# Next layer's weights in a six-layer stack: the cast to their high part moves from VectorE to ScalarE, and four groups of loads are issued one step later

## The reference, cut to what matters

```python
def attn_layer(x, Wqkv, qs, ksc, Wo):
    qkv = x @ Wqkv                      # 16 heads of 64
    q = l2norm(q) * qs
    k = l2norm(k) * ksc
    q = q * cos * scale + rotate_half(q) * sin * scale
    k = k * cos * inv + rotate_half(k) * sin * inv
    out = local_attention(q, k, v)      # windows of 32, each looks at 64 keys
    return out @ Wo
for i in range(DEPTH):                  # DEPTH = 6
    x = attn_layer(shift_tokens(x), Wqkv[i], q_scale[i], k_scale[i], Wo[i]) + x
    x = ffn_layer(shift_tokens(x), ln_g[i], ln_b[i], W1[i], b1[i], W2[i], b2[i]) + x
```

## Time and profile before

| what | us |
|---|---|
| median of three runs | 1199.79 (1198.54 to 1201.1) |
| the profiled execution, its own time | 1197.58 |
| its span, first to last instruction | 1195.8 |
| PE busy | 1116.0 (93%) |
| VectorE busy | 930.1 (78%) |
| ScalarE busy | 839.9 (70%) |
| GpSimd busy | 684.2 (57%) |
| mean granted TensorE clock | 0.983 of full speed |

### The profile page before, as it was taken

How to read it: one execution, slowest core, us unless ns; L and a number is a source line. 1 busy time by engine, 2 the same in 40 slices (tenths; PEclk the granted TensorE clock), 3 DMA queues, 4 the chain that set the end, 5 groups by cost and what they waited for, 6 DMA issues and landing times. The chain is left out here.

```text
span 1195.8 us, 26412 instructions
## 1 busy us (share of the span) xinstructions
PE 1116.0 (93%) x9694; PEld 711.2 (59%) x9694; DVE 930.1 (78%) x1367; ACT 839.9 (70%) x1340; POOL 684.2 (57%) x546
## 2 busy tenths in 40 slices
PE   9877889998868999999999999999999999999997
PEld 3222367785324776766666676666666676666662
DVE  3999868775538887888888787888888788888853
ACT  5655465664445787788877887788877887787853
POOL 2999655442526665755666565755656565755520
PEclk9989999999969999999999999999999999999999
DMA  5332162100303643535334443535344453544320
GB/s 168 107 96 96 36 194 74 39 14 1 106 0 88 156 115 82 130 96 150 95 102 120 124 121 82 129 99 154 87 104 119 122 126 79 127 103 110 92 69 18
DMA packets 81223, 117.48 MB, mean 98 GB/s; under 512 B 26003, under 2 KB 32594, under 8 KB 80714
## 3 DMA queue, kind: packets, MB, share of 16 engines
q1 hardware_dynamic: 80586, 115.03, 36.1%
q10 hardware_dynamic: 512, 0.80, 0.2%
HBM read 41.12 MB, written 0.72 MB: 35 GB/s over the span
## 5 line engine op out<-in xcount | busy, mean ns | idle before, releaser
L2061 POOL TENSOR_TENSOR st_sq_sum<-h 128x512 f32<-128x512 f32 x96 | 122.3, 1274 | 209.7 <-ACT h L1704 209.3
L2065 POOL TENSOR_TENSOR mo_w<-mo_w,x 128x512 f32<-128x512 f32 x96 | 123.1, 1282 | 105.6 <-DVE x L1876 105.5
L1890 DVE SCALAR_TENSOR_TENSOR st_turned<-banks,mo_w 128x1024 f32<-128x1024 f32 x96 | 117.5, 1224 | 66.7 <-POOL mo_w L2067 34.2
L1704 ACT ACTIVATE h<-banks 128x512 f32<-128x512 f32 x192 | 114.5, 597 | 74.2 <-PE banks L1491 70.0
L1511 PEld LDWEIGHTS banks<-st_wv,stream 128*128 128x128 f32 x768 | 101.6, 193 | 44.0 <-issue 43.2
L1552 PEld LDWEIGHTS banks<-st_p_blocks,st_vs 128*64 128x64 f32 x1536 | 81.1, 137 | 76.1 <-issue 76.1
L2067 POOL TENSOR_TENSOR mo_w<-mo_w,x 128x512 f32<-128x512 f32 x96 | 124.0, 1292 | 0.0
L1750 ACT ACTIVATE st_p_blocks<-banks 64x512 f32<-64x512 f32 x192 | 112.0, 583 | 9.3 <-PE banks L1540 6.9
L2074 POOL TENSOR_TENSOR mo_w<-st_prob,st_ri 128x512 f32<-128x512 f32 x96 | 100.9, 1051 | 19.6 <-DVE st_ri L1990 19.6
L1528 PE MATMUL banks<-st_k_blocks,st_qT 128*32 128x128 f32 x3072 | 103.8, 276 | 6.7 <-DMA st_k_blocks<-st_turned 6.6
L1511 PE MATMUL banks<-st_wv,stream 128*128 128x128 f32 x768 | 102.3, 277 | 0.0
(11 more groups left out here) (294 smaller groups left out, 2743.4 us busy)
## 6 DMA issues: line engine op xcount, KB each, us to landing
st_qT<-st_turned SPq DMA_DIRECT2D x192, 128.0 KB, 2.3
st_k_blocks<-st_turned SPq DMA_DIRECT2D x384, 64.0 KB, 2.0
st_vs<-st_vn SPq DMA_DIRECT2D x96, 192.0 KB, 2.5
ma_b_rows<-state_rows SPq DMA_DIRECT2D x32, 256.0 KB, 3.6
st_w_raw<-in_w_qk SPq DMA_DIRECT2D x12, 512.0 KB, 4.9
st_vs<-st_vn SPq DMA_DIRECT2D x96, 48.0 KB, 2.1
mo_w_all<-gate_rows SPq DMA_DIRECT2D x1, 3072.0 KB, 11.5
st_wv<-in_w_v SPq DMA_DIRECT2D x12, 256.0 KB, 3.0
```

The costliest lines, as they stand in the source:

```text
L1704: A(sq[:, part, :], ps[:, part, :], ACT.Square).then_inc(sq_done.sem, 1)
L1890: v.scalar_tensor_tensor(turned[:, h % 4], NORM_BANK.unsqueeze(1).to_broadcast([P, 2, SEQ]), 1e12, cos_part[:, which], ALU.min, ALU.mult). ...
L2061: nc.gpsimd.tensor_tensor(sq_sum[:], sq[:, 0, :], sq[:, 1, :], ALU.add).then_inc(sq_summed.sem, 1)
L2065: nc.gpsimd.tensor_tensor(cos_part[:, which, 0, :], cos_part[:, which, 0, :], sin_part[:, 1, :], ALU.subtract).then_inc(add_done.sem, 1)
```

## The change

SyncE issues four groups of loads one step later: FFN weights in step 6 and no longer 5, query and key weights with `rope_scale` in step 4 and no longer 3, half of the value weights in step 12 and no longer 11, half of the output weights in step 14 and no longer 13. The cast to the high part is ScalarE's and no longer VectorE's, in the same steps 7 to 14; on ScalarE it stands behind the copy of the output and ahead of the scaled table. Within a step the place of the loads, behind `place_heads` and `shift_values`, is as it was.

```diff
-                if t == 5:
+                if t == 6:
                     if res2_done.any(turn, 0):
                         sp.wait_ge(*res2_done.at(turn, 0))
                     load_ffn(turn)
                 if not s.last:
-                    if t == 3:
+                    if t == 4:
 
                         sp.wait_ge(*w_split.at(turn, PARTS))
                         for half in range(2):
                             places.load_qk(sp, d, turn + 1, half)
                         sp.wait_ge(*scaled_done.at(turn, 4))
                         places.load_scale(sp, d, turn + 1)
-                    if t == 11:
+                    if t == 12:
                         sp.wait_ge(*v_done.at(turn, 12))
                         places.load_v(sp, d, turn + 1, 0)
-                    if t == 13:
+                    if t == 14:
                         sp.wait_ge(*wo_step.at(turn, 12))
                         places.load_wo(sp, d, turn + 1, 0)
...
+        def high_weights(s, i, ahead):
+            ac.wait_ge(*proj_in.at(s.turn, 32 * ahead + 32))
+            A(w_high[:, i, :], w_raw[:, i, :], ACT.Copy).then_inc(w_high_done.sem, 1)
...
                 if t >= 0 and s.unit(t):
                     copy_out(s, t)
+                if PARTS - 1 <= t < 2 * PARTS - 1 and not s.last:
+                    high_weights(s, t - PARTS + 1, 1)
                 if 4 <= t < 8 and not s.last:
                     scale_table(s, (t - 4) // 2, t % 2, 1)
...
-        def high_weights(s, i, ahead):
-
-            dv.wait_ge(*proj_in.at(s.turn, 32 * ahead + 32))
-            v.tensor_copy(w_high[:, i, :], w_raw[:, i, :]).then_inc(w_high_done.sem, 1)
-
...
-                if t >= PARTS - 1 and t < 2 * PARTS - 1 and not s.last:
-                    high_weights(s, t - PARTS + 1, 1)
```

## The result

The change makes the kernel 3.55% slower: a median of 1242.4 us over four runs (1239.1 to 1244.2) against 1200.0, a ratio of 1.0355 with a 95% interval of 1.0331 to 1.0379. The forecast was 1235, with 1221 to 1247 as its range; the loss is 42.4 us where 35.4 were forecast. The profiled execution took 1242.15 us with a span of 1240.4.

The account below looks back on a forecast made before the run. TensorE, busy 93% of the span, was taken to set the pace. Table wait 31.3 plus clock 9.0, less cast 4.0 and keys' waits 0.9, gave +35.4 us on 1199.8: 1235 us, range 1221 to 1247.

Parts of the forecast that it names:

- The wait of the first table: ScalarE's first scaled table in step 4 waits for the later `rope_scale` load, and PE stands still: 31.3 us lost.
- the 1.4 that turn 0 gets back: Turn 0, step 5: PE's 1.37 us wait for keys that came behind the megabyte goes away.
- The landing: Time from issue of the `rope_scale` load until its data is there: taken as 4.7 us, lower bound 2.0.
- K + 7.4: SyncE's step 4: `rope_scale` is issued 7.4 us after K, the first issue for keys; in turn 1 at 551.2.
- The clock: PE behind each standstill: granted clock falls to half, 1.8 us lost each time, 9.0 us in five turns.
- The cast: Forty casts go from VectorE to ScalarE, shortening PE's steps: 0.8 us per turn, 4.0 us gained, between 0 and 5.
- the 0.44: Step 9 with the cast on VectorE takes 9.29 us against 8.85 for step 1 without: 0.44 us per turn.
- The other loads: The other moved loads: 0.9 us of waits for keys gained; value, output and FFN weights cost nothing by themselves.
- Landing in 2.0 us: Rival, `rope_scale` in step 4: the small load doesn't queue behind the megabyte; +22, 1222 us, chance 0.10.
- More stalls, or a longer landing: Rival: step 6 overruns or step 8's keys come late, or landing is 6.6; +10, 1245 us, both 1255; chance 0.12.
- Faster: Rival, ScalarE's step 4: the table doesn't wait and only gains are left; -6, 1194 us, chance 0.04.
- A clock that holds: Rival: the wait is there but PE's clock doesn't fall, the rest as forecast; +26, 1226 us, chance 0.08.

Follow-up runs that it names:

- the filler: 34 spare bf16 matmuls put in step 5 of turns 0 to 4, ahead of the wait for the sum of squares, against the kernel after: 1233.7 us, ratio 1.0275.

## Why the prediction was right, and which terms were mis-sized

**The wait of the first table: right in mechanism, too small.** Forecast were standstills of 6.7 us in four turns and 31.3 us net of the 1.4 that turn 0 gets back; PE stood for 40.5, or 39.1 on that footing. Two terms of the queue were under-sized. The landing was taken at 4.7 and was 5.5 to 6.2, 6.7 us more over five turns, although the range of 4.6 to 6.6 held it. The second half of the megabyte was later, too (6.5 us to landing in turn 1, where it had been 4.9). That the keys in flight ahead of the megabyte do this is a guess: the small load alone, behind the same keys and values, landed in 1.8 to 1.9 us in four of five turns. And the issue was put at K + 7.4; it came at K + 7.4 in turn 0, but at 8.5, 8.0, 8.3 and 8.2 in the others, 3.3 us more together, since the eight issues for keys (turns 1 and 3) or the two for values (turns 2 and 4) took longer, up to 1.1 us more than the 4.97 and 1.3 that I had taken. A third term went the other way: I had made PE's standstill as long as the squares are late, and it was some 0.5 us shorter each time (8.9 against 9.4 in turn 1), 2.3 in all. Together that is 7.7 of the 7.8 us between the 32.7 of standstill in my working and the 40.5 measured. I had argued that the eight issues were slow before because of the megabyte ahead of them; with no megabyte there they were slow all the same (6.04 us in turn 1, where it had been 5.86). What slows them stays open.

**The clock: right in size, and surer in my text than its row allowed.** 9.0 forecast, 9.0 to 9.4 in the profile of the kernel after, 8.8 between the medians with and without the filler. I had argued from one fall behind a wait of 2.31 us, and the same wait left the clock alone in five of twelve profiles; that a standstill of 7 to 9 us brings it down every time is what these runs show. The Trainium skill's advice (TensorE: Matmul & The Clock Gate, "Why this matters for your kernels") to leave no idle gaps between bursts is borne out by the earlier trace rows and by the windows after the change.

**The cast: right in sum, wrong in place.** 4.0 forecast, 3.3 between the medians with the cast alone, 5.2 between the loads alone and the kernel after. The step that failed is the claim that ScalarE has next to no idle time in steps 8 to 10, so that part of the 0.44 is given back. In the kernel before it was idle for 2.0, 0.5 and 1.8 us in them (turn 1), and step 9, the tightest, kept its whole 0.44 (8.85 us). What was given back was in step 11, which I had not looked at: the cast stood ahead of the stream's high part, and step 12 became 0.41 us longer. Step 0, which I had not counted, gained 0.25; the two misses nearly cancel, and that the sum came out right is luck in this part.

**The other loads: right that they gain little, one cover missed.** No wait for keys is left in step 5 of turn 0 or step 6. That is worth 2.6 us in the steps of the kernel after, where I had 0.9 and the 1.4 of turn 0. What the later loads gain without the move of `rope_scale` is not shown. Between the medians of the run with the cast alone and of the one with `rope_scale` in step 3 lie 3.7 us, but their intervals meet, and in their profiles the stack takes the same time (1193.8 - 373.3 = 820.5 and 1190.4 - 369.7 = 820.7): those two executions differ ahead of it, in code that is the same. I had looked at who reads each moved load, and not at who stands behind it in the queue a step later: the values of unit 6. Absent in the kernel after, this wait shows as soon as the large one is gone.

**The rivals.** Landing in 2.0 us: false in this order, and it is what happens in most turns (1.8 to 1.9 us) when the megabyte is not ahead; that run took 1215.9 us where the rival's arithmetic gave 1222 for a later issue. The Trainium skill (DMA: Bandwidth & Descriptors, "Queues, rings and completion order") says that an engine takes descriptors in ring order; by that rule a small load waits for the large one ahead of it, and the pair 6.2 and 1.8 us agrees. More stalls, or a longer landing: there was one stall per turn and step 8's keys came in time, but the other half of that rival, priced at 1.9 us more per turn, nearly came true. So 1242.4 us lies just outside the 1230 to 1242 of the forecast on its own and nearer to this rival's 1245; the whole range held it. Faster: only without the move of `rope_scale`. A clock that holds: no.

## What to carry to other kernels

When a group of loads is moved, ask of each its own first reader: the megabyte had three steps to spare and the 2 KB issued with it had none, and their move turned a change that is some 7 us faster without it into one that is 42 us slower. Put a small load that somebody waits for ahead of the large ones of its group, and read a DMA queue as a list in which whatever is in front, in issues and in bytes, is part of the latency. A stall of 3 us or more on a TensorE that has no other idle time cost the stall and then the clock in every such case here; and once it is removed, look at the waits again, since it may have hidden the next.

## What the runs showed that I had not expected

- Behind one and the same wait of 2.3 us for keys the clock fell in seven of twelve profiled executions and held in five.
- The time to landing of one and the same 2 KB load was mostly 1.8 to 1.9 us with no megabyte just ahead (3.2 to 3.5 in some turns), 4.6 to 4.9 behind it in step 3 of turns 1 to 4 of the kernel before, and 5.5 to 6.2 behind it in step 4 of the kernel after (5.4 to 7.2 over the three runs that have this order).
- Moving the megabyte between steps 3, 4 and half to 5 only moved which transfer comes late (keys, values, keys); each cost PE 0.2 to 1.5 us in some turns and nothing in others.
